# Reordering a cross-attention pair: contexts behind the scores, weights turned ahead of the key sums

## The chip, the cores and the metric

The kernel runs on one core of a Trainium2 chip. The metric is the time of one execution on the device, in microseconds (us), as the median of several runs. The engines are named as the profile names them: PE is TensorE (PEld its weight loads), DVE is VectorE, ACT is ScalarE, POOL is GpSimd, SP is SyncE.

## What is computed

One gated layer in float32 on 1024 tokens (16 sequences of 64) of width 256: cross-attention to a context of the same 16 by 64 rows of width 128, then causal self-attention, then a mixture of 16 experts with a shared one. Sixteen heads of width 128 in either attention. The change touches the cross-attention alone:

```python
q = rmsnorm((layernorm(x) @ Wq).reshape(B, Sq, H, D), gq)
k = rmsnorm((ctx @ Wk).reshape(B, Skv, H, D), gk)
v = (ctx @ Wv).reshape(B, Skv, H, D)
attn = softmax(einsum('bqhd,bkhd->bhqk', q, k) / sqrt(D))
out = einsum('bhqk,bkhd->bqhd', attn, v).reshape(B, Sq, H * D) @ Wo
x = x + tanh(g_xattn) * out
```

## The kernel before

The work is a list of six stages: cross-attention ("a"), self-attention ("b") and experts ("m"), each for two halves of 512 tokens. A stage "a" or "b" is eight pairs of heads, numbered 0 to 7 here; half 0 and half 1 of stage "a" are the sixteen cross pairs. Every engine has its own program for a pair (`cross_pair` on PE, ACT, DVE and POOL), an order written out by hand, and the engines meet in semaphores that count up. Nothing on an engine overtakes what stands before it.

The order is a software pipeline over three pairs. While pair u is attended to, pair nxt is projected, and the pair prev is multiplied out. A float32 product is made as three fast ones (hi*hi, hi*lo, lo*hi), so each operand has a hi part, a rounded copy, and a lo part, the rest. For weights DVE makes the hi part and POOL the rest (`split_queries`, `split_keys`; all of POOL's rests are recorded on L1452), for two pairs ahead ("after").

What PE does for pair u, with its lines. `norm_q` (L634): sums of squared queries, 32 small matmuls into bank_q. `scores` (L659): 32 matmuls of 128*64 tiles into bank_s. `project_keys` (L512 into bank_k, three matmuls a head in the cross stage). `project_queries` (L512, six matmuls, into bank_q and bank_v). `context_values` (L680): sixteen matmuls of 64*128 tiles, the attention weights of prev times the context, into bank_p and bank_t. `output` (L539): pv times the folded weights vo, into acc. `value_out` (L623), half 0 alone: Wv times Wo of the pair, into bank_k. `norm_k` (L645): sums of squared keys of nxt, into bank_p, from sq_k_hi and sq_k_lo. `turn_attn` (L667): four transposes of attn into bank_t. There are six banks beside acc, so an order is also an order of the banks: contexts may write bank_p only when ln_k has been read from it, `project_keys` may write bank_k for head 1 only when kt of head 0 has been read.

The other engines' part. ACT: `root_k`, `log_q`, `root_q`; `take_k` (L905) copies bank_k to kt; `square_k` (L909) makes sq_k and its rounded copy sq_k_hi; `take_context_values` (L957) makes pv_hi; `square_q` (L900) squares bank_q or bank_v; `exponentials` (L939); `take_rows` (L944) copies bank_t to rows_t; `log_k` (L925) takes the logarithm of the key sums. DVE: `scale_scores` (L1219, L1222, L1228), `split_context_values` (L1204, pv_lo), `subtract_max` (L1233), `take_q` (L1249, bank_q times gqk into qt, behind the square of the same head), the hi parts of weights (L1261, L1273), `normalise` (L1239, L1241, L1243: attn), then the same for head 1, and in half 0 vo_lo (L1299). POOL: sq_k_lo, the rest of the squared keys (`split_squares`), and the rests of weights (`split_head`).

The next step's tokens are prepared in pieces beside the pairs (`plan_of`). Half 0: pair 4 takes statistics and the norm (DVE), pair 5 turns the tokens (PE L699, ACT `take_tokens` L864 to xt_hi, DVE L1162 to xt_lo). Half 1: pair 2 statistics and norm, pair 3 mean squares on ACT (L847) and their root, pair 4 the scaling on DVE (L1152, L1156), pair 5 the turn (L866, L1166). The pieces of a slot stand in `prepare` on PE and ACT and in `prepare_piece` on DVE: on DVE the first slot's piece stands between `normalise` and `take_q` of head 1, on ACT behind `exponentials`. What PE must wait for after a turn of tokens is the list `held`.

SP loads the weights of a pair again (`reload_a1`) when POOL has made the rests of the pair before it, head by head, since those are the last readers of raw_a1.

Of the kernel before, what the change touches and what calls it, by code (L numbers as in the profile page):

```python
# [186 lines left out]
def flamingo_layer(nc, x, ctx_t, ctx, head_a, head_b, pair_v, chunk_m, small, out, shared_units):  # L187
# [35 lines left out]
    with ExitStack() as stack:  # L223
# [148 lines left out]

        def turn_banks(u):

            return (bank_p, bank_s if u.kind == "b" else bank_t)

        def query_bank(u, h):
            return bank_v if u.kind == "a" and h else bank_q
# [126 lines left out]
        def _(pe):  # L505
# [225 lines left out]
            def release(held):  # L731
                for semaphore, value in held:
                    pe.wait_ge(semaphore, value)

            def cross_pair(u):

                prev, nxt = u.prev(), u.next()
                norm_q(u)
                scores(u)
                if nxt.kind == "a":  # L740
                    if prev and prev.weighs_values:
                        pe.wait_ge(A["vo_lo"], prev.n)
                    project_keys(nxt, 0)
                else:
                    pe.wait_ge(A["ln_q"], u.n)
                    project_queries(nxt, 0)
                if prev:
                    pe.wait_ge(A["ln_k"], u.n)
                    context_values(prev)
                if nxt.kind == "a":  # L750
                    project_keys(nxt, 1)
                    pe.wait_ge(A["ln_q"], u.n)
                    project_queries(nxt, 0)
                else:
                    project_keys(nxt, 0)
                if prev:
                    output(prev, 0)
                held = prepare(u)
                if nxt.kind == "a":
                    project_queries(nxt, 1)  # L760
                if prev:
                    output(prev, 1)
                if nxt.kind == "a":
                    if u.weighs_values:
                        value_out(u)
                    release(held[:1])
                    if not prev:
                        pe.wait_ge(A["ln_k"], u.n)
                    norm_k(nxt)
                    release(held[1:])  # L770
                    turn_attn(u)
                else:
                    project_queries(nxt, 1)
                    turn_attn(u)
                    project_values(nxt, False)
                    context_values(u)
                    project_keys(nxt, 1)
                    project_values(nxt, True)
# [58 lines left out]
        def _(act_e):  # L837
# [103 lines left out]
            def take_rows(u):  # L941

                act_e.wait_ge(A["t_done"], u.n)
                nc.scalar.activation(rows_t[:].rearrange("p n h q -> p h n q"), by_tile(bank_t[:]), ACT.Copy)\  # L944
                    .then_inc(A["attn_t"], 1)
# [37 lines left out]
            def cross_pair(u):  # L983

                prev, nxt = u.prev(), u.next()
                if prev:
                    take_rows(prev)
                root_k(u)
                log_q(u)
                root_q(u)  # L990
                if nxt.kind == "a":
                    take_k(nxt, 0)
                    square_k(nxt, 0, sq_k, A["sq_k"])
                if prev:
                    take_context_values(prev)
                if nxt.kind == "a":
                    take_k(nxt, 1)
                    square_k(nxt, 0, sq_k_hi, A["sq_k_hi"])
                    square_q(nxt, 0)
                else:  # L1000
                    take_k(nxt, 0)
                exponentials(u)
                prepare(u)
                if nxt.kind == "a":
                    square_k(nxt, 1, sq_k, A["sq_k"])
                    square_k(nxt, 1, sq_k_hi, A["sq_k_hi"])
                    square_q(nxt, 1)
                    if u.weighs_values:
                        take_value_out(u)
                    if u.very_first:  # L1010
                        split_context(1)
                    prepare(u, 1)
                    log_k(nxt)
                else:
                    take_rows(u)
                    take_v(nxt, False)
                    take_context_values(u)
                    take_k(nxt, 1)
# [430 lines left out]
        def _(pool):  # L1449
# [51 lines left out]
            def cross_pair(u):  # L1501
                nxt = u.next()
                after = nxt.next()
                if nxt.kind == "b":
                    split_values(nxt)
                for h in range(2):
                    if nxt.kind == "a":
                        split_squares(nxt, h)
                    split_head(after, h)
                if u.very_first:  # L1510
                    split_context(1)
# [39 lines left out]
            split_head(start, 1)  # L1551
            for h in range(2):
                split_squares(start, h)
                split_head(start.next(), h)
            bodies = {"a": cross_pair, "b": self_pair, "m": chunk}
            for kind, half in STAGES:
# [71 lines left out]
```

## Time and profile before

| | us |
|---|---|
| median of 3 runs | 703.63 (701.22 to 703.67) |
| profiled execution, its own time | 702.43 |
| its span, first to last instruction | 700.5 |
| cross-attention, 16 pairs | 22 to about 235 |
| TensorE busy / GpSimd busy | 674.3 / 304.0 |
| mean granted TensorE clock | 0.994 |

The span is shorter than the time of the same execution by what lies around it, 1.9 us. A busy time is the sum of an engine's instructions, whose ends on TensorE are modelled, so that neighbours overlap a little; the time from one group's start to the next group's start is what a group costs. A wait in the table of waits is idle time of an engine, put down to the instruction that released it.

### The profile page before, as it was taken

Reading aid. Unit: us, or ns where it says so; the run is one execution under the profiler, and the core shown is the slowest. Engines: PE = TensorE matmul, PEld = TensorE weight load, DVE = VectorE, ACT = ScalarE, POOL = GpSimd, SP = SyncE. Lnnn points to the kernel's source line nnn. Section 1 sums busy time; section 2 is a strip of 40 time slices with the busy share of each in tenths; the row PEclk is TensorE's granted clock in tenths of the full one; section 3 lists DMA queues with packets and bytes.
Section 4 is the critical chain, followed back from the end, with each engine's and each line's share of the span. In section 5 each row is a group of like instructions: output and inputs, shape, how many; then the busy total and the mean of one; then the engine's idle time right before and its main releaser. Section 6 shows DMA issues by size and latency. Waiting matters only on the chain.

```text
span 700.5 us, 14630 instructions
## 1 busy us (share of the span) xinstructions
PE 674.3 (96%) x5422; PEld 587.0 (84%) x5422; DVE 460.2 (66%) x881; ACT 343.2 (49%) x688; POOL 304.0 (43%) x372
## 2 busy tenths in 40 slices
PE   7799999999999999999999989999999999999997
PEld 6588888888787898898889888888888888888886
DVE  4457777769666667686666748766555788655555
ACT  4567667667665333433344423335446634444442
POOL 4443433534334343333333324433554566555543
PEclk9899999999999999999999999999999999999999
DMA  6421121110101122221113221111333232333332
GB/s 201 152 69 46 48 84 53 36 35 24 35 12 32 46 76 91 70 68 61 61 61 93 74 62 53 55 31 39 97 90 91 77 100 73 101 101 92 90 90 91
DMA packets 35849, 50.07 MB, mean 71 GB/s; under 512 B 4048, under 2 KB 22864, under 8 KB 35792
## 3 DMA queue, kind: packets, MB, share of 16 engines
q1 hardware_dynamic: 35504, 49.03, 23.7%
q8 instruction: 39, 0.64, 0.4%
q10 hardware_dynamic: 288, 0.26, 0.1%
q14 instruction: 18, 0.15, 0.1%
HBM read 48.22 MB, written 1.05 MB: 70 GB/s over the span
## 4 chain that ended last, share of the span: by engine, by line
PE 84%; DVE 6%; ACT 4%; POOL 3%; issue 2%; DMA 0%; SPq 0%; DVEq 0%; POOLq 0%; ACTq 0%
PE acc L539 19%; PE bank_k L512 14%; PE bank_q L512 13%; PE bank_v L613 6%; PE bank_v L512 6%; PE bank_s L659 5%; PE bank_s L512 4%; PE bank_p L690 3%; PE bank_p L645 2%; PE bank_p L680 2%; PE bank_q L634 2%; PE bank_t L690 2%; POOL sq_k_lo L1452 2%; PE bank_t L667 2%; ACT sq_q L900 1%
## 5 line engine op out<-in xcount | busy, mean ns | idle before, releaser
L539 PE MATMUL acc<-wo_hi,pv_hi 128*128 128x256 f32 x328 | 94.4, 288 | 1.5 <-DVE pv_lo L1322 1.5
L1452 POOL TENSOR_TENSOR sq_k_lo<-sq_k,sq_k_hi 128x512 fp32r<-128x512 f32 x32 | 48.7, 1523 | 104.3 <-ACT sq_k_hi L909 104.3
L539 PE MATMUL acc<-wo_lo,pv_hi 128*128 128x256 f32 x328 | 92.6, 282 | 0.0
L539 PE MATMUL acc<-wo_hi,pv_lo 128*128 128x256 f32 x328 | 92.2, 281 | 0.0
L905 ACT ACTIVATE kt<-bank_k 128x512 f32<-128x512 f32 x64 | 38.3, 599 | 71.6 <-PE bank_k L512 71.5
L1452 POOL TENSOR_TENSOR wq_lo<-raw_m,wq_hi 128x256 fp32r<-128x256 f32 x50 | 43.5, 870 | 59.4 <-DVE wq_hi L1280 56.0
L539 PEld LDWEIGHTS acc<-wo_hi,pv_hi 128*128 128x128 f32 x328 | 61.5, 188 | 5.4 <-DVE pv_lo L1322 2.4
L539 PEld LDWEIGHTS acc<-wo_lo,pv_hi 128*128 128x128 f32 x328 | 61.8, 188 | 1.9
L539 PEld LDWEIGHTS acc<-wo_hi,pv_lo 128*128 128x128 f32 x328 | 62.0, 189 | 0.0
L981 ACT ACTIVATE pv_hi<-rows_t 128x512 fp32r<-128x512 f32 x50 | 31.6, 633 | 61.1 <-DVE rows_t L1318 60.2
L1322 DVE TENSOR_TENSOR pv_lo<-rows_t,pv_hi 128x512 fp32r<-128x512 f32 x50 | 36.7, 735 | 36.3 <-ACT pv_hi L981 36.3
L512 PE MATMUL bank_q<-xt_hi,wq_hi 128*128 128x512 f32 x146 | 59.3, 406 | 0.0
L1452 POOL TENSOR_TENSOR wk_lo<-raw_m,wk_hi 128x256 fp32r<-128x256 f32 x50 | 41.8, 835 | 36.2 <-ACT wk_hi L1055 36.1
L512 PE MATMUL bank_q<-xt_hi,wq_lo 128*128 128x512 f32 x146 | 57.4, 393 | 0.0
L512 PE MATMUL bank_q<-xt_lo,wq_hi 128*128 128x512 f32 x146 | 57.4, 393 | 0.0
L1311 DVE TENSOR_TENSOR r_k<-ln_k,unit_w 128x512 f32<-128x512 f32 x44 | 33.3, 757 | 36.5 <-ACT ln_k L973 36.2
L1452 POOL TENSOR_TENSOR wq_lo<-raw_b,wq_hi 128x256 fp32r<-128x256 f32 x32 | 24.4, 764 | 71.8 <-DVE wq_hi L1264 71.8
L1452 POOL TENSOR_TENSOR wv_lo<-raw_v,wv_hi 128x512 fp32r<-128x512 f32 x16 | 20.7, 1293 | 61.1 <-DVE wv_hi L1287 61.1
L512 PE MATMUL bank_k<-xt_hi,wk_hi 128*128 128x512 f32 x114 | 45.1, 395 | 0.0
L512 PE MATMUL bank_k<-xt_lo,wk_hi 128*128 128x512 f32 x114 | 44.9, 393 | 0.0
L512 PE MATMUL bank_k<-xt_hi,wk_lo 128*128 128x512 f32 x114 | 44.7, 392 | 0.0
L1452 POOL TENSOR_TENSOR wo_lo<-raw_m,wo_hi 128x256 fp32r<-128x256 f32 x50 | 38.2, 764 | 10.4 <-ACT wo_hi L1049 10.4
(198 smaller groups left out, 1983.4 us busy)
## 6 DMA issues: line engine op xcount, KB each, us to landing
raw_m<-in_chunk_m SPq DMA_DIRECT2D x50, 256.0 KB, 2.7
raw_a<-in_head_a SPq DMA_DIRECT2D x48, 192.0 KB, 2.5
raw_b<-in_head_b SPq DMA_DIRECT2D x32, 256.0 KB, 3.0
raw_m<-in_chunk_m SPq DMA_DIRECT2D x50, 128.0 KB, 2.1
raw_v<-in_pair_v SPq DMA_DIRECT2D x16, 256.0 KB, 2.9
raw_b<-in_head_b SPq DMA_DIRECT2D x32, 128.0 KB, 2.1
out<-xs SPq DMA_DIRECT2D x4, 256.0 KB, 2.3
xs<-in_x SPq DMA_DIRECT2D x6, 128.0 KB, 3.1
```

What stands on the lines that cost most here:

```text
L512: last = nc.tensor.matmul(bank[:], w[:, cols], m(k), start=n == 0, stop=n == 3 * chunks - 1)
L539: last = nc.tensor.matmul(acc[t // 2][:, (t % 2) * D:(t % 2 + 1) * D], w[:, tok], m, start=begins and n == 0, stop=True, skip_group_check= ...
L613: last = nc.tensor.matmul(bank_v[:, b * PAIR:(b + 1) * PAIR], m, w[:, cols], start=n == 0, stop=n == 3 * KD - 1)
L634: last = nc.tensor.matmul(bank_q[s * SEQ:(s + 1) * SEQ, h * NT + t:h * NT + t + 1], sq_q[:, h, b * SEQ:(b + 1) * SEQ], ones[:], start=True ...
L645: last = nc.tensor.matmul(bank_p[:], ones_of[:, s, :], keys, start=first, stop=final)
L659: last = nc.tensor.matmul(bank_s[s * SEQ:(s + 1) * SEQ, g * SEQ:(g + 1) * SEQ], qt[:, h, tok], kt[:, h, tok], start=True, stop=True)
L690: last = nc.tensor.matmul(value_bank(h)[:, n * P:(n + 1) * P], vs[:, n, h * P:(h + 1) * P], attn_t[:, h * NT + n, :, :], start=True, stop= ...
L905: nc.scalar.activation(kt[:, h], bank_k[:], ACT.Copy).then_inc(stage["kt"], 1)
L981: nc.scalar.activation(pv_hi[:, u.parity], hh, ACT.Copy).then_inc(M["hh_hi"], 1)
L1311: nc.vector.tensor_tensor(gu, gs, weights, ALU.mult).then_inc(M["weighted"], 1)
L1322: nc.vector.tensor_tensor(pv_lo[:, u.parity], hh, pv_hi[:, u.parity], ALU.subtract).then_inc(M["hh_lo"], 1)
L1452: nc.gpsimd.tensor_tensor(lo, raw, hi, ALU.subtract).then_inc(signal, 1)
```

## The change

Three engines' orders change; no instruction is added or removed. `turn_banks` gives the cross stage's token turn its two banks the other way round. TensorE: the context products of prev come directly behind the scores, then keys 0, queries 0, keys 1 of nxt; the weights are turned ahead of the key sums. In the last cross pair, which projects for a self-attention pair, contexts also come first. ScalarE: `take_context_values` stands ahead of `take_k`; both squares of head 0's keys come together; `square_q` of head 0 moves behind the exponentials and behind the piece; `take_rows` of the pair itself stands at the end of the pair, ahead of `log_k`, where before it stood at the start of the next pair, behind `log_k`. GpSimd: sq_k_lo of both heads ahead of both heads' weight rests. DVE's order is not touched.

```diff
--- before.py
+++ after.py
@@ -372,7 +372,7 @@
 
         def turn_banks(u):
 
-            return (bank_p, bank_s if u.kind == "b" else bank_t)
+            return (bank_t, bank_p) if u.kind == "a" else (bank_p, bank_s if u.kind == "b" else bank_t)
 
         def query_bank(u, h):
             return bank_v if u.kind == "a" and h else bank_q
@@ -737,22 +737,16 @@
                 prev, nxt = u.prev(), u.next()
                 norm_q(u)
                 scores(u)
+                if prev:
+                    pe.wait_ge(A["ln_k"], u.n)
+                    context_values(prev)
                 if nxt.kind == "a":
                     if prev and prev.weighs_values:
                         pe.wait_ge(A["vo_lo"], prev.n)
                     project_keys(nxt, 0)
-                else:
-                    pe.wait_ge(A["ln_q"], u.n)
-                    project_queries(nxt, 0)
-                if prev:
-                    pe.wait_ge(A["ln_k"], u.n)
-                    context_values(prev)
-                if nxt.kind == "a":
-                    project_keys(nxt, 1)
-                    pe.wait_ge(A["ln_q"], u.n)
-                    project_queries(nxt, 0)
-                else:
-                    project_keys(nxt, 0)
+                pe.wait_ge(A["ln_q"], u.n)
+                project_queries(nxt, 0)
+                project_keys(nxt, int(nxt.kind == "a"))
                 if prev:
                     output(prev, 0)
                 held = prepare(u)
@@ -764,11 +758,11 @@
                     if u.weighs_values:
                         value_out(u)
                     release(held[:1])
+                    turn_attn(u)
+                    release(held[1:])
                     if not prev:
                         pe.wait_ge(A["ln_k"], u.n)
                     norm_k(nxt)
-                    release(held[1:])
-                    turn_attn(u)
                 else:
                     project_queries(nxt, 1)
                     turn_attn(u)
@@ -983,25 +977,20 @@
             def cross_pair(u):
 
                 prev, nxt = u.prev(), u.next()
-                if prev:
-                    take_rows(prev)
                 root_k(u)
                 log_q(u)
                 root_q(u)
-                if nxt.kind == "a":
-                    take_k(nxt, 0)
-                    square_k(nxt, 0, sq_k, A["sq_k"])
                 if prev:
                     take_context_values(prev)
+                take_k(nxt, 0)
                 if nxt.kind == "a":
+                    square_k(nxt, 0, sq_k, A["sq_k"])
+                    square_k(nxt, 0, sq_k_hi, A["sq_k_hi"])
                     take_k(nxt, 1)
-                    square_k(nxt, 0, sq_k_hi, A["sq_k_hi"])
-                    square_q(nxt, 0)
-                else:
-                    take_k(nxt, 0)
                 exponentials(u)
                 prepare(u)
                 if nxt.kind == "a":
+                    square_q(nxt, 0)
                     square_k(nxt, 1, sq_k, A["sq_k"])
                     square_k(nxt, 1, sq_k_hi, A["sq_k_hi"])
                     square_q(nxt, 1)
@@ -1010,9 +999,10 @@
                     if u.very_first:
                         split_context(1)
                     prepare(u, 1)
+                take_rows(u)
+                if nxt.kind == "a":
                     log_k(nxt)
                 else:
-                    take_rows(u)
                     take_v(nxt, False)
                     take_context_values(u)
                     take_k(nxt, 1)
@@ -1503,9 +1493,10 @@
                 after = nxt.next()
                 if nxt.kind == "b":
                     split_values(nxt)
+                if nxt.kind == "a":
+                    for h in range(2):
+                        split_squares(nxt, h)
                 for h in range(2):
-                    if nxt.kind == "a":
-                        split_squares(nxt, h)
                     split_head(after, h)
                 if u.very_first:
                     split_context(1)
@@ -1551,6 +1542,7 @@
             split_head(start, 1)
             for h in range(2):
                 split_squares(start, h)
+            for h in range(2):
                 split_head(start.next(), h)
             bodies = {"a": cross_pair, "b": self_pair, "m": chunk}
             for kind, half in STAGES:
```

## Rows read from the trace of the kernel before

**Rows 1.** The page, first part: busy us, share of the span, instructions.

```profile
PE 674.3 (96%) x5422; PEld 587.0 (84%) x5422; DVE 460.2 (66%) x881; ACT 343.2 (49%) x688; POOL 304.0 (43%) x372
```

**Rows 2.** Waits from 20 to 245 us: us, times, longest.

```profile
PE bank_p L645 <- POOL sq_k_lo L1452: 8.3, 9, 2.4
...
PE bank_k L512 <- DVE vo_lo L1299: 1.1, 1, 1.1
...
PE bank_k L512 <- ACT kt L905: 0.8, 1, 0.8
```

**Rows 3.** The chain that ended last: start, us, what.

```profile
36.47 1.03 PE bank_q L634 x32
...
74.94 1.03 PE bank_q L634 x32
...
102.65 1.03 PE bank_q L634 x32
...
153.38 1.03 PE bank_q L634 x32
...
165.91 1.03 PE bank_q L634 x32
...
179.62 1.03 PE bank_q L634 x32
...
192.17 1.03 PE bank_q L634 x32
...
218.81 1.03 PE bank_q L634 x32
```

**Rows 4.** Timeline, PE, half 1, pair 1: start, us, instruction [idle before].

```profile
154.26 1.13 PE L659 MATMUL bank_s<-kt,qt 128*64 128x64 f32 x32
155.32 0.50 PE L512 MATMUL bank_k<-ctxt_hi,wk_hi 128*128 128x512 f32 x1
155.66 0.39 PE L512 MATMUL bank_k<-ctxt_lo,wk_hi 128*128 128x512 f32 x1
155.89 0.40 PE L512 MATMUL bank_k<-ctxt_hi,wk_lo 128*128 128x512 f32 x1
156.22 0.37 PE L680 MATMUL bank_p<-rows_t,ctx_sb 64*128 64x128 f32 x1
...
157.31 0.50 PE L512 MATMUL bank_k<-ctxt_hi,wk_hi 128*128 128x512 f32 x1
...
164.28 0.50 PE L645 MATMUL bank_p<-sq_k_hi,ones_of 128*128 128x512 f32 x1 [0.32 <-POOL sq_k_lo L1452]
...
165.31 0.60 PE L667 MATMUL bank_t<-sm,attn 128*128 128x128 f32 x4
```

**Rows 5.** Timeline, ACT, DVE and POOL, the same pair.

```profile
159.69 0.60 ACT L900 ACTIVATE sq_q<-bank_q 128x512 f32<-128x512 f32 x1
...
160.32 0.69 DVE L1249 TENSOR_TENSOR qt<-bank_q,gqk 128x512 f32<-128x512 f32 x1 [0.32 <-ACT sq_q L900]
...
162.30 0.79 DVE L1243 TENSOR_TENSOR attn<-ex,ex_inv 128x512 f32<-128x512 f32 x1
...
162.49 1.74 POOL L1452 TENSOR_TENSOR sq_k_lo<-sq_k,sq_k_hi 128x512 fp32r<-128x512 f32 x1
```

**Rows 6.** The timeline, DVE and ACT, half 1, pairs 3 and 4.

```profile
168.59 0.68 DVE L1219 TENSOR_TENSOR sc_sub<-bank_s,r_k 128x512 f32<-128x512 f32 x1
...
173.22 0.41 ACT L847 ACTIVATE junk<-ys 128x256 f32<-128x256 f32 x1
...
175.38 0.63 ACT L909 ACTIVATE sq_k<-kt 128x512 f32<-128x512 f32 x1
...
192.38 0.68 DVE L1249 TENSOR_TENSOR qt<-bank_v,gqk 128x512 f32<-128x512 f32 x1
```

**Rows 7.** Timeline, PE: the key sums ahead of the first pair.

```profile
20.05 0.80 PE L645 MATMUL bank_p<-sq_k_hi,ones_of 128*128 128x512 f32 x1 [2.00 <-POOL sq_k_lo L1452]
```

**Rows 8.** Windows: busy PE, PEld, DVE, ACT, POOL, then PEclk, DMA share, GB/s.

```profile
20.00:28.00 8.00, 7.18 (x72) 5.57 (x72) 2.29 (x5) 2.55 (x6) 1.15 (x2) 0.57 0.73 225
```

## The prediction

> **What bounds the kernel now.** I read the page first: TensorE is busy for 674.3 of 700.5 us and GpSimd for 304.0 [rows 1]. So only two things can shorten the span: TensorE waits that end, and seams between its groups of matmuls that get cheaper. Next the waits between 20 and 245 us, the sixteen cross pairs that the diff touches. There TensorE waited 8.3 us, in 9 places, for the rest of the key squares (sq_k_lo), 1.1 us for vo_lo and 0.8 us for kt [rows 2]. One of the nine, 2.0 us, lies in the start-up ahead of the first pair [rows 7]. That leaves about 8 us at stake in all. Then the chain of waits, where the query sums (L634) open each pair: it gives the lengths. The first pair ends at 36.47. An ordinary pair of half 0 takes 12.82 (38.47 for three). The two from 74.94 to 102.65 take 27.71, so the one that turns tokens (pair 5) takes 14.89. In half 1 an ordinary pair takes 12.53, pair 3 (mean squares) 13.71, and pairs 5 (token turn) and 6 together 26.64 [rows 3].
>
> **TensorE's order, costed.** I take the pair whose scores start at 154.26. Between scores and contexts stand keys 0 (155.32 to 156.22, 0.90 us), and keys 1 follow the contexts (0.80) [rows 4]. Matmuls of one shape follow each other in 0.23 (155.66 to 155.89), so three cost 0.69; the rest, about 0.1 each, is the seam to another tile shape. After the change one key group stands behind the contexts (0.80) and one behind the queries (0.69): 1.49 for 1.70. The seam from scores (128*64) straight to contexts (64*128) is nowhere in this trace. Its bounds, counted beyond what leaving the scores costs now, are -0.1, if column and row tiles run on without a seam, and 0.2, if both seams of today are paid and a little more. I take 0, since every seam seen costs about 0.1 whichever way it goes. The trace's seams are all to or from the full array; the Trainium skill (TensorEngine Tiling (Array Packing), Key Properties) says that changing the tiling mode drains the engine. By that rule the direct step still pays one drain, and two drains become one; no row here shows the direct step.
>
> **Keys behind queries, and the key sums last.** So output 0 starts 0.2 us sooner, at about 159.3. The key sums, now between the turn and the query sums, I put at 1.05 (164.28 to 165.31 is 1.03 after a wait; behind value_out it is about 1.1) and the turn at 0.52 [rows 3, 4]. Together an ordinary pair without a wait loses 0.28: six pairs of half 0, **-1.7 us**.
>
> **Both squares first on GpSimd.** Today sq_k_lo of head 1 starts at 162.49 behind two weight splits, lasts 1.74 and lets the key sums go at 164.28 [rows 4, 5]. Afterwards it starts as soon as its square is there, about 162.3, and ends near 163.8, while the sums stand a turn later, at 164.4. This wait goes. The weight splits that it passes end some 2.5 us later, at about 164.6 for head 0; their readers are the next pair's keys and queries, past 168, and the two reloads of raw_a1 on SP's queue, whose data are cast only behind the next pair's queries. I cost them at nothing; without that cover it would be up to 2 us a pair.
>
> **What is late next: the weights.** The change puts the square of queries 0 behind the exponential on ScalarE. Today it starts at 159.69, the qt product on DVE at 160.32, and attn ends at 162.30 + 0.79 = 163.09 [rows 5], over a microsecond before it is turned (165.31). DVE's order is untouched: that product, two casts, then the normalising. Afterwards ScalarE takes kt of head 1 at 159.4, the exponential 0.5 later, the square at 160.4, so DVE multiplies at 161.05 and, 2.77 on as today, attn ends at 163.8 to 163.9. TensorE would be at the turn at 163.6 to 163.7. It waits 0.1 to 0.3 for the weights. With 0.52 and 1.05 behind, the next pair opens at 165.4 for 165.83: -0.42 each for four pairs of half 1 (0, 1, 2 and 4), **-1.7**. Pair 6 comes to the same 12.1. In half 0 value_out (0.68) covers the late weights.
>
> **Where ScalarE has more in front of that square,** the change loses.
> - Half 1, pair 3. Pair 2's attn ends 0.8 later, with it the statistics and the norm behind it on DVE, so the first scaling starts at 169.4 for 168.59 [rows 6], though the pair opened 0.4 sooner. The split contexts are done 3.4 later, at 172.8; output 0 waits 1.4 for them. The shifted scores follow at 173.4, the exponential, then the mean squares (173.22 to 175.38, 2.16 [rows 6]), which now stand ahead of the square: 176.1. Attn at 179.5, turn and sums, next pair at 181.15. Length 15.7 for 13.71: **+2.0**.
> - Half 1, pairs 5 and 6. In pair 4 the scaling of tokens stands between attn and qt of head 1 (192.38 [rows 6]), which ends 13.4 into the pair; now 14.25, when scores are due at 13.1: 1.15 wait. Then two token copies (1.1) go ahead of the square and two token splits ahead of the turn, which waits for the first: some 2 us. Length 16.1, and with pair 6 28.2 for 26.64: **+1.6**.
> - Half 0, pair 5. Keys 0 wait for vo_lo about 1.1 as before, output 0 waits 0.4, the turn 1.2. 16.4 for 14.89: **+1.5**.
>
> **The ends.** First pair: keys 1 behind the queries need not wait for kt (0.8), and the last wait ends on attn instead of sq_k_lo: **-1.1**. Last pair: contexts go out 1.4 sooner and so do pv_hi and pv_lo, one seam and a wait of 0.4 go, queries and keys stand still: **-0.6**.
>
> **Sum.** -1.7 - 1.7 - 1.1 - 0.6 + 2.0 + 1.6 + 1.5 = 0.0. Against the profiled execution (span 700.5, time 702.43) that is 702.4; the median of the runs shown is 1.2 higher, so 703.6. Two things that I bounded move it: the seam, fourteen times -0.1 to +0.2, -1.4 to +2.8; and the late pairs, whose 5.1 I take to be known to about 2 either way, since they add up some ten waits from rows of other pairs.
>
> **Rivals.** Bound of all: 0.5% of this time, 3.5 us, is about what a measurement can tell from no change.
> 1. *The late weights hide.* Were attn ready in time in the ordinary and the late pairs too, the GpSimd waits (6.3), vo_lo's or kt's (about 1) and 13 times 0.2 of seams would go: about 694. Against it: the square stands behind the exponential in the diff, and DVE's cast order is unchanged. A weaker form, in which the late pairs cost half, gives 703.6 - 2.6 = 701.0, and with a free seam (-1.4) 699.6. For all that ends over 0.5% faster, 0.15.
> 2. *TensorE's clock falls in the longer gaps.* Place: the 1.4 and 2 us gaps of pair 3 and pair 5 in half 1. After the 2.0 us gap in the start the granted clock was 0.57 over 20 to 28 us, its lower level of 1.2 GHz for most of them [rows 7, 8], though not after the longest wait for sq_k_lo, 2.4 us in the first pair [rows 2]. The price is 8 times 0.43 = 3.4 us a time: 707.0 once, 710.4 twice. It decides if either gap leaves a low clock behind; one is enough with any loss beside it. 0.17 for all that ends over 0.5% slower.
> 3. *No more than an exchange,* the forecast: one wait for another, within 0.5%. The case in which the orders do nothing, since both wait ends at the same time anyway, gives the same number. 0.68.
>
> **How the numbers follow.** Forecast 703.6 from the sum. The range leaves a tenth on each side: below, a free seam and late pairs at a lower price give 699.5; above, one fall of the clock with a little of the dear seam gives 708.0.
>
> **What would show it.** Right: no wait of the key sums for sq_k_lo in the pairs, waits of the turn (L667) for attn of 0.1 to 0.3 in half 1 and over 1 us in the three late pairs; ordinary pairs of 12.5 and 12.1; contexts straight behind the scores with a gap of about 0.1. Wrong: late pairs that keep their length (then faster), contexts that cost 0.3 more (slower), a granted clock under 0.9 past 170 us (slower), or key sums that still wait for GpSimd.

## The result, and the profile after

The changed kernel takes **710.41 us** (median; 708.78 to 711.37), the kernel before 702.95 (701.22 to 703.67) beside it: ratio 1.0103, 95% interval 1.0071 to 1.0135. The forecast of 703.6 was wrong and its range, to 708.0, too low. The profiled span grew from 700.5 to 708.5 us, and the mean granted clock fell from 0.994 to 0.985.

From the page of the changed kernel, the busy times and the granted clock in forty slices:

```profile
PE 677.2 (96%) x5422; PEld 593.4 (84%) x5422; DVE 460.7 (65%) x881; ACT 346.2 (49%) x688; POOL 304.0 (43%) x372
...
PEclk9789999999998999999999999999999999999999
```

TensorE, with the same instructions, is 2.9 us busier than before [rows 1]: they ran slower for a while. The slices that show it are the second, the third and the thirteenth; the fall in the second, in the start-up, the kernel before has too. The waits of the stretch of the cross pairs (20 to 252 us), changed kernel; columns: us in total, times, longest:

```profile
PE bank_t L667 <- DVE attn L1233: 7.3, 7, 2.5
...
PE bank_t L667 <- DVE xt_lo L1156: 2.3, 1, 2.3
...
PE bank_p L645 <- POOL sq_k_lo L1442: 1.9, 1, 1.9
...
PE bank_t L667 <- DVE xt_lo L1152: 1.1, 1, 1.1
...
PE acc L539 <- DVE pv_lo L1194: 1.4, 2, 1.2
```

Of the nine waits for sq_k_lo [rows 2] the one in the start-up is left [rows 7]; the other eight are gone, as forecast. In their place stand waits of the turn (L667), longer together. The openings of pairs in the chain of waits of the changed kernel (start, us, engine, tile, line):

```profile
105.55 1.03 PE bank_q L634 x32
...
143.06 1.03 PE bank_q L634 x32
...
155.45 1.03 PE bank_q L634 x32
...
183.75 1.03 PE bank_q L634 x32
...
212.50 1.80 PE bank_q L634 x32
...
227.79 1.03 PE bank_q L634 x32
```

An ordinary pair of half 1 takes 12.39 (143.06 to 155.45) where it took 12.53 [rows 3]. At 212.50 the opening lasts 1.80 for 1.03, and so it does at 35.82: there TensorE runs at half rate. The scores of the first self-attention pair start at 243.97 for 236.09, so the whole loss, 7.9 us, arises in the sixteen cross pairs. Their three stretches of lower clock, changed kernel (columns: us, then busy time and instructions of PE, PEld, DVE, ACT, POOL, then granted clock, DMA share, GB/s):

```profile
21.00:28.00 7.00, 7.00 (x73) 6.16 (x74) 2.76 (x4) 3.54 (x7) 1.00 (x2) 0.51 0.71 203
34.00:42.00 8.00, 8.00 (x91) 6.77 (x90) 3.56 (x7) 2.90 (x7) 3.15 (x5) 0.57 0.19 52
212.00:219.00 7.00, 7.00 (x84) 6.11 (x83) 2.34 (x5) 2.63 (x6) 1.14 (x2) 0.51 0.01 2
```

Each is about 6.8 us at the lower level, 1.2 GHz, and costs 3.4 us of the full clock. The first is the one before has too [rows 8]. The second follows a 2.45 us wait of the first pair's turn, the third the 2.26 us wait of the turn in half 1's pair 5. Behind the longest gap, 2.50 us in pair 3, the clock stayed up. The three waits:

```profile
33.75 0.66 PE L667 MATMUL bank_t<-sm,attn 128*128 128x128 f32 x4 [2.45 <-DVE attn L1233]
...
182.16 0.66 PE L667 MATMUL bank_t<-sm,attn 128*128 128x128 f32 x4 [2.50 <-DVE attn L1233]
...
210.53 0.65 PE L667 MATMUL bank_t<-sm,attn 128*128 128x128 f32 x4 [2.26 <-DVE xt_lo L1156]
```

An ordinary pair of half 1 on the timeline, changed kernel (start, duration, engine, line, tiles, shape; in brackets the idle time before and its releaser):

```profile
143.94 1.13 PE L659 MATMUL bank_s<-kt,qt 128*64 128x64 f32 x32
145.00 0.37 PE L680 MATMUL bank_p<-rows_t,ctx_sb 64*128 64x128 f32 x1
...
146.10 0.51 PE L512 MATMUL bank_k<-ctxt_hi,wk_hi 128*128 128x512 f32 x1
...
149.67 0.62 ACT L933 ACTIVATE ex<-sc_sub 128x512 f32<-128x512 f32 x1
150.19 0.59 ACT L894 ACTIVATE sq_q<-bank_q 128x512 f32<-128x512 f32 x1
...
150.81 0.69 DVE L1239 TENSOR_TENSOR qt<-bank_q,gqk 128x512 f32<-128x512 f32 x1 [1.62 <-ACT sq_q L894]
...
151.96 1.29 POOL L1442 TENSOR_TENSOR sq_k_lo<-sq_k,sq_k_hi 128x512 fp32r<-128x512 f32 x1 [1.55 <-ACT sq_k_hi L903]
...
152.71 1.09 DVE L1233 TENSOR_TENSOR attn<-ex,ex_inv 128x512 f32<-128x512 f32 x1
...
153.22 1.18 POOL L1442 TENSOR_TENSOR wq_lo<-raw_a,wq_hi 128x256 fp32r<-128x256 f32 x1
```

Scores to contexts take 1.06, contexts to keys 1.10: the new seam costs what the old ones did. The Trainium skill (TensorEngine Tiling (Array Packing), Key Properties) says that a change of tiling mode drains the array, so the direct step would still pay one drain. The trace agrees, as leaving the scores did not get cheaper than before (155.32 - 154.26 = 1.06 in [rows 4]). The square and qt come where they were forecast (qt 7.75 into the pair, 161.05 - 153.38 = 7.67 by the forecast), but attn takes 1.09 us for 0.79, and the turn waits 0.48.

**Look at who was first.** attn starts while GpSimd's sq_k_lo is running. That ends at 153.25, attn 0.55 later. Then GpSimd's wq_lo, begun inside attn, ends 0.59 behind attn's end. Before, only the short rest wk_lo was running when attn began:

```profile
162.07 0.47 POOL L1452 TENSOR_TENSOR wk_lo<-raw_a,wk_hi 128x128 fp32r<-128x128 f32 x1
```

It ends at 162.54, and attn 0.55 later, at 163.09. The sq_k_lo begun inside attn took 1.74 us [rows 5] and ended 1.14 beyond attn's end. The two take turns.

### The profile page after: what moved, and what is told of

Read it like the earlier page. It is cut to its first block, busy times and chain, and to the rows that moved or that the text cites. A ratio compares the mean times of both kernels' runs of the same rounds, so it can differ in the third digit from the quotient of the medians.

```text
span 708.5 us, 14630 instructions
## 1 busy us (share of the span) xinstructions
PE 677.2 (96%) x5422; PEld 593.4 (84%) x5422; DVE 460.7 (65%) x881; ACT 346.2 (49%) x688; POOL 304.0 (43%) x372
## 4 chain that ended last, share of the span: by engine, by line
PE 81%; DVE 11%; ACT 5%; issue 2%; DMA 0%; POOL 0%; SPq 0%; DVEq 0%; POOLq 0%; ACTq 0%
PE acc L539 19%; PE bank_k L512 14%; PE bank_q L512 13%; PE bank_v L613 6%; PE bank_v L512 5%; PE bank_s L659 5%; PE bank_s L512 4%; PE bank_p L690 3%; PE bank_p L680 2%; PE bank_q L634 2%; PE bank_t L690 2%; PE bank_p L645 2%; PE bank_t L667 2%; DVE attn L1233 1%; DVE ex_sum L1229 1%
## 5 line engine op out<-in xcount | busy, mean ns | idle before, releaser
L1442 POOL TENSOR_TENSOR sq_k_lo<-sq_k,sq_k_hi 128x512 fp32r<-128x512 f32 x32 | 41.2, 1287 | 121.6 <-ACT sq_k_hi L903 121.6
```

What stands on the lines that cost most here:

```text
L1442: nc.gpsimd.tensor_tensor(lo, raw, hi, ALU.subtract).then_inc(signal, 1)
```

## The experiments

All kernels but those with fillers compute the same as the kernel they start from with the same instructions; a filler multiplies zeros into a bank that is overwritten before it is read, so it adds nothing to the result. The kernel before, run beside them each time, had medians of 703.2 to 703.3. e1, e3 to e6, e11 and e12 ask what each part of the change costs; e2 and e7 to e10 what is left once the clock is held.

**e1: the changed kernel with the square back ahead of the exponential** (ScalarE alone).

```diff
+                if nxt.kind == "a":
+                    square_q(nxt, 0)
                 exponentials(u)
                 prepare(u)
                 if nxt.kind == "a":
-                    square_q(nxt, 0)
                     square_k(nxt, 1, sq_k, A["sq_k"])
```

> The changed kernel with one thing put back: on ScalarE the square of queries 0 stands ahead of the exponential and of the piece again. Theory A (the late weights cost the gaps, and the gaps cost the clock): attn is ready about 0.5 us sooner in an ordinary pair, so the turn's 0.48 us waits in half 1 go (pairs of 11.9 for 12.39), the 2.50 of pair 3 and most of the 2.26 of pair 5 go too, and without gaps of two microseconds the granted clock stays at its full level past 30 us: 15 us less than the changed kernel in all, 694 to 697. Rival B (TensorE's new order or the later weight rests cost the time, not the square): 705 or more, gaps ahead of the turn as before. Rival C (the clock falls whatever the gaps): the gaps go, but low stretches near 35 and 212 us stay, 700 to 702.

Measured: 702.44 us (697.29 to 703.8), ratio 0.9963 [0.9931, 0.9996]. The late square costs 8.0 us by the medians (710.41 - 702.44), and 5 us between runs of one clock (at 0.987 e1 takes 703.56 to 703.8, the changed kernel 708.78). Less came back than expected. Pairs 3 and 5 shrank to 14.5 and 14.0, and their gaps of 2.50 and 2.26 us are gone, but the first pair's gap of 2.45 us stays, with a low clock behind it, and a shorter fall follows two waits of 1.17 and 1.02 us in pair 3 (columns as above):

```profile
34.00:42.00 8.00, 8.00 (x90) 6.87 (x91) 3.70 (x7) 2.81 (x6) 3.28 (x5) 0.57 0.20 52
181.00:185.00 4.00, 4.00 (x76) 3.88 (x74) 0.96 (x2) 1.58 (x4) 0.86 (x2) 0.58 0.35 98
```

The turn of an ordinary pair still waits 0.48, too. The timeline of e1 in such a pair:

```profile
148.83 0.69 DVE L1240 TENSOR_TENSOR qt<-bank_q,gqk 128x512 f32<-128x512 f32 x1 [1.09 <-ACT sq_q L894]
...
150.50 1.29 POOL L1443 TENSOR_TENSOR sq_k_lo<-sq_k,sq_k_hi 128x512 fp32r<-128x512 f32 x1 [1.54 <-ACT sq_k_hi L903]
...
150.73 1.61 DVE L1234 TENSOR_TENSOR attn<-ex,ex_inv 128x512 f32<-128x512 f32 x1
```

The pair opened at 141.61, so attn starts 9.12 into it and ends at 10.73; in the changed kernel it starts at 9.65 (152.71 - 143.06) and ends at 10.74. It starts half a microsecond sooner and ends at the same time, 0.55 behind sq_k_lo in both (151.79 to 152.34 here). So sq_k_lo's end decides when attn ends, and moving the square alone can't free the turn.

**e2: the changed kernel, the gaps filled** ahead of two turns (first pair; half 1, pair 5), 8 matmuls each.

```diff
+            def fill(u, n):
+                pe.wait_ge(A["raw"], u.n)
+                for _ in range(n):
+                    nc.tensor.matmul(bank_s[:], zeros[:, 0:P], zeros[:], start=True, stop=True)
...
+                    if (u.half, u.i) == (0, 0) or (u.half, u.i) == (1, 5):
+                        fill(u, 8)
                     release(held[:1])
                     turn_attn(u)
```

> The changed kernel with eight matmuls of zeros (128x512, into the scores' bank once it has been read; about 0.23 us each, 1.85 in all) ahead of the turn in two pairs, the first of half 0 and pair 5 of half 1, where TensorE sat idle for 2.45 and 2.26 us anyway. They compute nothing and fit inside the gaps. Theory A (the idle stretch makes the clock fall): no low clock behind either, pair 1 of half 0 in 12.56 for 15.11 and pair 6 of half 1 in 12.4 for 15.29: 5.4 us less than the changed kernel, about 705. Rival B (the many small matmuls behind the gap, not the gap, make it fall): the low stretches stay, 710.

Measured: 705.73 (704.29 to 707.78), ratio 1.0036 [1.0016, 1.0056]; 4.7 us below the changed kernel. The same two stretches in e2 (columns as above):

```profile
34.00:42.00 8.00, 8.00 (x106) 6.86 (x106) 5.47 (x10) 5.49 (x11) 3.77 (x6) 1.00 0.19 53
212.00:219.00 7.00, 7.00 (x49) 6.12 (x46) 5.23 (x11) 5.98 (x11) 1.93 (x2) 1.00 0.00 0
```

No order is changed here, only idle time filled, and the clock is at its full level in both. That shows the clock as a cause of its own. Pair 5 keeps its length (16.29), so the fillers hide nothing else.

**e3 and e4: one part of the change alone, on the kernel before.** e3 takes only GpSimd's order:

```diff
-                for h in range(2):
-                    if nxt.kind == "a":
-                        split_squares(nxt, h)
+                if nxt.kind == "a":
+                    for h in range(2):
+                        split_squares(nxt, h)
+                for h in range(2):
                     split_head(after, h)
```

> The kernel before with GpSimd's part of the change alone: both key-square rests ahead of the weight rests. Theory A: the rest of head 1's squares is ready about 0.8 us sooner, the key sums' waits of 0.3 to 0.6 in half 1 go and the first pair's 2.36 becomes about 1.5; those of pairs 3 and 5, which hang on ScalarE, stay: 3 us less than before, about 699.8. Rival B (the later weight rests are missed, by TensorE or by the reloads of the raw weights): 703 or more, with new waits for wq_lo or wk_lo.

Measured: 703.73 (701.74 to 707.53), ratio 1.0015 [0.9993, 1.0038], about 4 above the expectation. Ordinary pairs of half 1 gain even more than the waits promise (11.96 for 12.53), but half 0's pair 5 and half 1's pairs 3 and 5 take 17.1, 15.3 and 14.8 where before has 14.9, 13.7 and 13.8: 4.8 us given back. Up to 1.7 of these are the clock's, in half 0's pair 5, behind a wait of 1.85 us for vo_lo; e3:

```profile
90.00:94.00 4.00, 4.00 (x23) 3.19 (x22) 2.35 (x4) 2.41 (x5) 0.00 (x0) 0.57 0.00 0
```

attn lasts 1.51 in its ordinary pairs, always with sq_k_lo begun first and always ending 0.55 behind it, and all of DVE behind attn is 0.7 later.

e4 takes only the turn ahead of the key sums, with `take_rows` at the pair's end and the token turn's banks:

```diff
                     release(held[:1])
+                    turn_attn(u)
+                    release(held[1:])
                     if not prev:
                         pe.wait_ge(A["ln_k"], u.n)
                     norm_k(nxt)
-                    release(held[1:])
-                    turn_attn(u)
```

> The kernel before with the turn of the weights ahead of the key sums alone (with the two banks of the token turn and the place of the copied rows that this needs); contexts, squares and GpSimd as before. attn is ready at 9.8 us into a pair, so the turn does not wait, and its 0.5 us lie in the time in which the key sums waited for GpSimd. Theory A: the 0.3 us waits of half 1 go, those of 1.4 and 2.4 shrink by 0.5: about 3.5 us less than before, 699.5. Rival B (the seams around the turn cost as much): 702 to 704.

Measured: 702.39 (699.53 to 703.75), ratio 0.9984 [0.9964, 1.0004]. Ordinary pairs of half 1 take 12.12, with no wait, though GpSimd's order is the old one: the turn ahead is enough. Half 0 stays at 12.83, pair 3 takes 14.69 (1.0 more).

**e5: the changed kernel with GpSimd's old order** (the diff of e3 taken back).

> The changed kernel with GpSimd's order put back (a head's key-square rest, then its weight rests); TensorE and ScalarE as changed. Theory A (attn, which DVE makes from two operands in SBUF, is held up by a GpSimd rest that runs beside it: 1.09 us in the changed kernel's ordinary pairs of half 1, 1.51 in the GpSimd part alone, 0.79 before): attn takes 0.8 us again, the turn waits about 0.2 for 0.48, but the rest of head 1's squares comes later and the key sums wait for it some 0.5: pairs of half 1 of 12.4 to 12.6, no gain in sum, 708 to 712, with gaps ahead of the turn in pairs 3 and 5 as in the changed kernel. Rival B (attn is long because of its place behind the square, whatever GpSimd does): attn stays at 1.1.

Measured: 718.21 (711.72 to 721.03), ratio 1.0215 [1.0172, 1.0257]; the profiled execution is the shortest of its runs, 711.72 at a clock of 0.987, the others lie at 0.973 to 0.980. attn is back to 0.79 on average, but with the late square the key sums wait 0.47 in each ordinary pair of half 1, which takes 12.80, and the granted clock is at its lower level over 6.8 us twice, from 179 and from 210. The highest expectation, 712, was too low for the median: the clock fell more often than in the profile. At the same clock, 0.987, the changed kernel takes 708.78. So GpSimd's order repaired about 3 us of what the late square did to the orders (one run of each at that clock), and the rest of the 7.8 us between the medians goes with the clock.

**e6: the changed kernel with both squares' places as before** (the diffs of e1 and e5 together), so only TensorE's two orders with the copies that go with them.

> The changed kernel with both of the others put back: the square of queries 0 ahead of the exponential, GpSimd's order as before. What is left is TensorE's order (contexts behind the scores, weights ahead of the key sums) and what it needs on ScalarE. Theory A: attn at 0.8 us and early, no wait of the turn outside the first pair; ordinary pairs 12.56 in half 0, 12.0 to 12.2 in half 1; pair 3 some 14.3, pair 5 of half 1 some 13.8; 700 to 701 with the clock low behind the first pair's gap, 697.5 where it isn't. Rival B (the square of keys 1, later now, keeps the key sums waiting as before): 702 or more.

Measured: **699.08** (694.2 to 702.38), ratio 0.9919 [0.9884, 0.9955], 3.4 us below e1, which differs by GpSimd's order alone. The group of attn from 40 to 252 us, sixteen of them (line, tiles, count, busy us, mean ns, idle before), in e6:

```profile
L1234 DVE TENSOR_TENSOR attn<-ex,ex_inv 128x512 f32<-128x512 f32 x16 | 12.9, 807 | 0.6
```

in e1:

```profile
L1234 DVE TENSOR_TENSOR attn<-ex,ex_inv 128x512 f32<-128x512 f32 x16 | 21.4, 1340 | 0.5
```

and in the changed kernel:

```profile
L1233 DVE TENSOR_TENSOR attn<-ex,ex_inv 128x512 f32<-128x512 f32 x16 | 16.9, 1055 | 0.6
```

The instruction is the same; what GpSimd does beside it is not. The key sums still wait for sq_k_lo in nine places, for 6.3 us in all where before has 8.3 [rows 2]; ordinary pairs take 12.56 and 12.30 nevertheless.

**e7: the kernel before, 8 fillers ahead of the very first key sums.**

```diff
+            for _ in range(8):
+                nc.tensor.matmul(bank_s[:], zeros[:, 0:P], zeros[:], start=True, stop=True)
             norm_k(start)
```

> The kernel before with eight matmuls of zeros more (1.85 us) in the start-up, where TensorE waits 2.0 us for the squares ahead of the first key sums. Theory A (idle time makes the clock fall, and a fall costs 2.5 to 3.5 us): no stretch at half clock from 20 to 27 us, the first pair in about 12 for 14.35, 3 us less than before: 700.3. Rival B (the clock falls there for another reason): the low stretch stays, 703.5.

Measured: 703.09 (698.96 to 706.0), ratio 0.9985 [0.9955, 1.0015]: no gain. In e7:

```profile
20.00:28.00 8.00, 7.22 (x87) 5.67 (x86) 3.34 (x5) 5.23 (x11) 2.19 (x3) 1.00 0.68 202
32.00:40.00 8.00, 8.00 (x91) 6.38 (x89) 2.17 (x4) 3.32 (x7) 1.83 (x3) 0.57 0.13 36
```

The start runs at full clock, and the fall comes one gap later, behind the first pair's wait of 2.37 us for sq_k_lo. In the kernel before, the like gap of 2.36 us left the clock up:

```profile
34.86 0.47 PE L645 MATMUL bank_p<-sq_k_hi,ones_of 128*128 128x512 f32 x1 [2.36 <-POOL sq_k_lo L1452]
...
32.00:40.00 8.00, 5.64 (x90) 4.39 (x90) 4.82 (x9) 4.59 (x10) 5.11 (x6) 1.00 0.33 98
```

One gap filled doesn't hold the clock for certain if the next is open. In three of e7's ten runs it did hold (0.999), and these took 698.96 to 699.72.

**e8: e6 with fillers** at the start (as e7) and ahead of the first pair's turn.

> The orders of TensorE alone (square and GpSimd put back), with eight matmuls of zeros in the start-up wait and eight ahead of the first pair's turn. Theory A: no low clock behind either, 3 us less than the same orders without them: 697 to 698, faster than both kernels by 0.7 to 0.8%. Rival B (the falls move elsewhere): 700 or more, with a low stretch behind another gap.

Measured: **695.96** (694.8 to 699.37), ratio 0.9895 [0.9853, 0.9937]: the fastest median, ahead of both kernels. Its best run (694.80) lies with e6's best three (694.2 to 694.84), so at full clock the fillers change little. That they make this case more frequent is likely but not shown: e8 has four runs, and its interval overlaps e6's. From the first pair to half 1's pair 5 the clock stayed up, e8:

```profile
28.00:200.00 172.00, 166.58 (x1770) 143.56 (x1770) 125.79 (x261) 119.31 (x240) 72.70 (x84) 1.00 0.17 52
```

**e9 and e10: both kernels with every long gap filled.** e9 is the kernel before with the fillers of e7 and these:

```diff
+                    if (u.half, u.i) in ((0, 0), (1, 3)):
+                        fill(u, 4 if u.half else 8)
                     release(held[:1])
                     if not prev:
                         pe.wait_ge(A["ln_k"], u.n)
                     norm_k(nxt)
```

> The kernel before with zero matmuls in its longest idle stretches: eight in the start-up wait, eight ahead of the first pair's key sums, four ahead of those of pair 3 of half 1. Together with the next kernel it parts what the orders cost from what the clock costs. Theory A: no low clock at all, the stretch from 20 to 27 us gone: 3 us less than before, 700 or a little under. Rival B (falls come whatever is filled): 703, with a low stretch elsewhere.

e10 is the changed kernel with those of e7 and these:

```diff
+                    fills = {(0, 0): 8, (0, 5): 4, (1, 3): 8, (1, 5): 8}
+                    if (u.half, u.i) in fills:
+                        fill(u, fills[u.half, u.i])
                     release(held[:1])
                     turn_attn(u)
```

> The changed kernel with zero matmuls in its idle stretches: eight in the start-up wait, and ahead of the turn eight in the first pair, four in pair 5 of half 0, eight in pairs 3 and 5 of half 1. Theory A: no low clock; what is left against the kernel before with its own gaps filled is the orders alone, by the pairs' lengths 2 to 3 us: 702 to 703 here for 700 there. Rival B (the orders cost all of the 7 us, the clock nothing): 707 or more.

Measured: e9 699.87 (699.04 to 701.45), ratio 0.9961 [0.9939, 0.9982]; e10 702.98 (700.87 to 704.71), ratio 0.9992 [0.9969, 1.0014]. The stretch of cross pairs in e9:

```profile
28.00:240.00 212.00, 206.77 (x2131) 174.97 (x2130) 150.82 (x303) 133.15 (x271) 86.97 (x97) 1.00 0.16 47
```

and in e10, with one more, in the experts' part:

```profile
28.00:240.00 212.00, 204.03 (x2135) 175.94 (x2134) 149.02 (x300) 135.40 (x270) 86.01 (x96) 1.00 0.17 49
416.00:420.00 4.00, 3.64 (x18) 3.67 (x19) 0.69 (x1) 0.81 (x2) 0.00 (x0) 0.57 0.53 175
```

The medians lie 3.1 us apart, the first self-attention scores in the profiles only 1.9 (235.11 for 233.23). The rest goes with falls like that one in the experts, which the diff doesn't touch; seven of the fourteen profiles have one between 410 and 430 us, e9's has none. The mean clock of each run shows it; here are times and clocks of single runs:

| kernel | its runs at 0.999 to 1.000 | its runs at a lower clock |
|---|---|---|
| e9 (before, filled) | 699.04 to 700.12, six | to 701.45 at 0.997 |
| e10 (changed, filled) | 700.87 to 701.81, three | 702.42 to 704.71, seven, at 0.998 to 0.995 |
| e6 | 694.2 to 694.84, three | to 702.38 at 0.987 |
| e1 | none | 697.29 at 0.997, 703.8 at 0.987 |
| changed | none | 708.78 at 0.987, 711.37 at 0.983 |

So at full clock the changed orders cost **1.9 us** (the median of e10's three, 701.43, less that of e9's six, 699.55), as the profiles say. Without fillers it comes out alike: at 0.987 the changed kernel takes 708.78, and the kernel before, in three of the runs beside the experiments, 706.18 to 707.38. The rows of e6 show what the clock alone does to one kernel: 8 us between 1.000 and 0.987.

**e11: contexts behind the scores alone, on the kernel before** (TensorE's first hunk, with ScalarE's copies in that order, the square still ahead of the exponential).

```diff
+                if prev:
+                    pe.wait_ge(A["ln_k"], u.n)
+                    context_values(prev)
                 if nxt.kind == "a":
                     if prev and prev.weighs_values:
                         pe.wait_ge(A["vo_lo"], prev.n)
                     project_keys(nxt, 0)
...
+                pe.wait_ge(A["ln_q"], u.n)
+                project_queries(nxt, 0)
+                project_keys(nxt, int(nxt.kind == "a"))
```

> The kernel before with the contexts directly behind the scores alone (TensorE's group order and what ScalarE reads in the same order; the square of queries 0 stays ahead of the exponential; turn, rows and GpSimd as before). Theory A: one seam less and two cheaper key groups, 0.26 us in each of six pairs of half 0; in half 1 the wait for sq_k_lo grows by about what the seams save, since the squares of keys 1 are read later (keys 1 now follow the queries): pairs of 12.5 to 12.8 there. 701.5 to 703.5. Rival B (the contexts' early place is what makes the changed kernel slow): 705 or more.

Measured: 702.4 (697.5 to 707.09), ratio 0.9977 [0.9934, 1.0019]. Half 0's ordinary pairs take 12.74 for 12.82, half 1's 12.73 for 12.53. The seam saves 0.24 up to value_out (10.28 into the pair for 10.52), and the key sums behind it wait longer for sq_k_lo (in half 1 0.77 each), which takes most of it back. By the medians neither of TensorE's orders is worth much alone (e4, e11); together (e6) the first makes work earlier and the second covers the wait that this opens. At full clock e11's three runs took 697.5 to 697.72, e6's 694.2 to 694.84 and the kernel before with its gaps filled (e9) 699.04 to 700.12: 2 us for the first order, 5 us for both.

**e12: the late square alone, on the kernel before.**

```diff
                     square_k(nxt, 0, sq_k_hi, A["sq_k_hi"])
-                    square_q(nxt, 0)
                 else:
                     take_k(nxt, 0)
                 exponentials(u)
                 prepare(u)
                 if nxt.kind == "a":
+                    square_q(nxt, 0)
                     square_k(nxt, 1, sq_k, A["sq_k"])
```

> The kernel before with one line of ScalarE moved as in the change: the square of queries 0 behind the exponential and the piece. Theory A (it only bites where the weights are turned early): in ordinary pairs attn ends some 0.5 us later and is still in time, because the turn stands behind the key sums; the square of keys 1 is 0.5 later and with it the rest on GpSimd, so the key sums wait 0.4 to 0.8 instead of 0.3; pairs 3 and 5 of half 1 lose 1 to 2 us each because the mean squares and the token copies stand ahead of the square and of DVE's work behind it: 706 to 709 in all. Rival B (TensorE never waits for it here): 703.5.

Measured: **720.1** (717.74 to 722.94), ratio 1.0247 [1.0177, 1.0316], 11 us above the highest expectation. It is the orders more than the clock: at 0.990 it takes 717.74 and 718.03, the kernel before 705.6. The waits of e12 and its timeline in a pair of half 0:

```profile
PE bank_p L645 <- POOL sq_k_lo L1452: 17.1, 15, 3.2
```

```profile
57.28 0.58 ACT L900 ACTIVATE sq_q<-bank_q 128x512 f32<-128x512 f32 x1
...
58.50 0.28 DVE L1261 CAST wq_hi<-raw_a 128x256 fp32r<-128x256 f32 x1
...
58.86 0.74 POOL L1452 TENSOR_TENSOR wq_lo<-raw_a,wq_hi 128x256 fp32r<-128x256 f32 x1 [1.00 <-DVE wq_hi L1261]
...
59.56 0.47 POOL L1452 TENSOR_TENSOR wk_lo<-raw_a,wk_hi 128x128 fp32r<-128x128 f32 x1
...
59.98 1.72 POOL L1452 TENSOR_TENSOR sq_k_lo<-sq_k,sq_k_hi 128x512 fp32r<-128x512 f32 x1
```

The square is late, so qt and the weight cast behind it on DVE are late, GpSimd waits 1.00 for that cast with head 1's squares queued behind it, and the key sums wait in every pair: 13.3 us for 12.82 in half 0, too.

## Why the prediction was wrong, point by point

What held:
- **Seam and order.** Ordinary pairs of half 0 lost 0.26 (12.56), forecast 0.28; the direct step costs nothing extra.
- **The key sums' wait** for sq_k_lo is gone from all pairs, and the new waits are where they were named: the turn in half 1, and pairs 5, 3 and 5.
- **The last pair** gained 1.1 (16.18 from its opening at 227.79 to the scores at 243.97, 17.28 before), forecast 0.6; the first, at full clock, 0.95 (11.30 in e10, 12.25 in e9), forecast 1.1.

What failed, in order of size:
- **The clock** (rival 2, at 0.17). The sum held no term for it, though the range reached to one more fall; there were two. A fall had nearly the right price (3.4 us of clock, 2.9 to 3.0 of time) and the wrong chance. Against the runs at full clock with the gaps filled, the changed kernel loses 9.0 us (710.41 - 701.43) and the one before 3.4 (702.95 - 699.55): 5.6 us of the 7.5 between them, and 1.9 are the orders'. In the profiles it is 6.0 of 7.9: the first self-attention scores come 8.9 sooner in e10 than in the changed kernel (three falls), 2.9 sooner in e9 than before (one fall). I held against it that the first pair's 2.4 us gap had left the clock up [rows 2]. e7 shows a fall behind that same gap. One gap without a fall, in one execution, was evidence of a chance, and I read it as a rule. I also looked for the gap in pairs 3 and 5 alone; one fall came behind the first pair, whose gap I had not put on the list. That the rival's "710.4 twice" is the measured time is partly luck: it counts two falls at 3.4 and nothing for the orders, where the runs show 6.0 and 1.9.
- **The late pairs,** forecast +5.1 (1.5, 2.0, 1.6), came to 2.05 (16.94), 2.2 (15.92) and, at full clock, 2.0 (16.29 and 12.37 in e2): 6.3.
- **Ordinary pairs of half 1,** forecast -0.42 each, gave -0.15. I wrote "attn ends 2.77 on as today" and costed the moved GpSimd rest by its readers alone, at nothing. It now starts ahead of attn instead of behind it, and attn's 0.79 became 1.09; in e1 1.61. The row that said so was in the prediction's own group: a sq_k_lo of 1.74 begun inside attn [rows 5], where one with nothing beside it takes 1.29. I wrote the 1.74 down and didn't ask what had made it so long.

The sum of the measured terms: 6 times -0.26, 4 times -0.15, -0.95, -1.1, +2.05, +2.2, +2.0, which is +2.0; e9 against e10 show 1.9. So the exchange was nearly even, as forecast (0.0), though by terms that were off both ways, and most of the loss is what happened to the clock behind gaps of TensorE.

**Whose part it is.** The late square on ScalarE has the largest part in both: put back it gives 8.0 us (e1), alone it costs 16.9 (e12), and with it stand the gaps of 2 us ahead of the turn in pairs 3 and 5 of half 1. The first pair's gap of 2.45 us stays without it (e1). GpSimd's order helps only where the square is late (710.4 with it, 718.2 without, e5); where the square is early it costs 3.4 by the medians (e1 against e6), and 1.7 between runs of one clock (at 0.987 e1 has 703.56 to 703.8, e6 701.68 and 702.38). TensorE's two orders are sound: 699.1 (e6), and 696.0 with fillers (e8). At full clock e6's 694.6 stands against 701.4 for the whole change (e10): what the late square and GpSimd's order cost together is 6.8 us.

Open: which gap lets the clock fall. In the profiles the falls of the cross pairs lie behind gaps of 1.6 to 3.2 us, in e1 behind two of about 1 us near each other. Gaps of 2.36 (before), 2.50 (changed) and 2.48 (e2) had none behind them. The falls differ between executions, too: e11 has runs of 697.5 at 1.000 and of 707.09 at 0.985, while the filled e9 spreads over 2.4 us. The short falls late in the experts' part were not studied.

## What to carry to other kernels

When an instruction is moved, ask what the other engine runs at its new time, as well as who reads its result: here the rest of the squares on GpSimd, made earlier, took its time from the one product on DVE that the path was waiting for. Count a new gap of two microseconds on TensorE as a chance of 1.7 or 3.4 us more, even where a like gap of the trace left the clock up; a few matmuls of zeros in the gaps bought most of that back (3.3 us in one kernel, 7.4 in the other, by the medians). And test the parts alone and together: the two orders that gave 0.2 to 0.3% each, within the noise, gave 0.8% together, once the parts that spoiled them were out.

## What the runs showed of the hardware

- **DVE and GpSimd take turns** where DVE multiplies two operands in SBUF (attn). In every cross pair of the kernel before, the changed one, e1, e3 and e6 in which a GpSimd rest was running when attn began, attn ended 0.54 to 0.56 us behind it, whatever its start; a rest begun inside attn ended 1.12 to 1.15 (128x512) or 0.58 to 0.61 (128x256) behind it. With nothing beside it attn took 0.69 (e1, half 1, pair 3, at 176.13). The neighbour's product with an operand in PSUM (qt) took 0.69 beside a rest, too. The Trainium skill (GPSIMD Engine Reference, 8. Key points) says that GpSimd shares its way to SBUF with DVE and that the two get in each other's way where DVE reads two operands from SBUF; the trace agrees, and in it the one that comes second waits for the other's end.
- **The clock.** In the cross pairs a stretch at the lower level lasted about 3.4 or 6.8 us and cost 1.7 or 3.4 of the full clock. With matmuls of zeros in the gaps ahead it stayed up: in the profiles of e8, e9 and e10 nothing fell in the cross pairs.
- **A fall costs less time than clock, and can come back one gap later.** Without two of the three falls (e2), 6.8 us of clock, the first self-attention scores come 5.95 us sooner (238.02 for 243.97). With the start's gap filled (e7) the second pair opens 2.8 us sooner than before (33.63 for 36.40), but the fall behind the next gap leaves 0.5 of it at the third (48.72 for 49.23).
